# Attention heads stacked by DMA inside SBUF instead of by 0/1 matmuls

## The reference, cut to what matters

```python
q = (x @ Wq.T).reshape(B, T, h, dh).transpose(0, 2, 1, 3)      # first layer; k and v alike
att = jnp.einsum('bhqd,bhkd->bhqk', q, k) / jnp.sqrt(jnp.float32(dh))
out = jnp.einsum('bhqk,bhkd->bhqd', jax.nn.softmax(att, axis=-1), v)
x = x + out.transpose(0, 2, 1, 3).reshape(B, T, D) @ Wo.T
```

## Time and profile before

| | us |
|---|---|
| median of 3 runs | 3458.74 (3458.63 to 3459.36) |
| span of the profiled execution | 3458.2 |
| first attention, loop over 4 batches | 48.3 to 552.9 |
| causal attention, loop over 4 batches | 2846.0 to 3340.0 |
| TensorE busy | 2971.3 |
| mean granted TensorE clock | 0.937 |

### The profile page before, as it was taken

The page is one execution under the profiler, slowest core; times in us unless marked ns, Lnnn a source line. Parts: engine busy times, 40 slices in busy tenths (PEclk is TensorE's granted clock), DMA queues, the critical chain, the costliest instruction groups (busy, mean ns, idle before and its releaser), DMA issues. The chain is left out here.

```text
span 3458.2 us, 45847 instructions
## 1 busy us (share of the span) xinstructions
PE 2971.3 (86%) x13906; PEld 2032.8 (59%) x13906; DVE 1702.4 (49%) x4581; ACT 1078.2 (31%) x1834; POOL 1115.2 (32%) x1189
## 2 busy tenths in 40 slices
PE   5888888999999999999899999999999537777762
PEld 3544546887556556788766666666666425455552
DVE  3464463666655655566432332333333546546545
ACT  2443454443011001444333233333232014333410
POOL 1111105776444444676622222222223002213210
PEclk9999999999999999999999999999999659988985
DMA  3000002000000000200100000000000000000000
GB/s 138 1 0 0 0 0 92 0 0 0 1 0 0 0 0 0 98 0 0 61 1 1 1 1 1 1 1 1 1 1 1 34 0 1 1 0 0 0 0 24
DMA packets 5276, 39.97 MB, mean 12 GB/s; under 512 B 160, under 2 KB 4256, under 8 KB 4384
## 3 DMA queue, kind: packets, MB, share of 16 engines
q1 hardware_dynamic: 5152, 38.43, 2.7%
HBM read 36.33 MB, written 2.10 MB: 11 GB/s over the span
## 5 line engine op out<-in xcount | busy, mean ns | idle before, releaser
L364 PE MATMUL banks<-moe_parts 128*128 128x512 f32 x1536 | 370.0, 397 | 12.2 <-POOL moe_parts L444 7.3
L1500 PE MATMUL banks<-xt,back 128*128 128x512 f32 x768 | 349.6, 599 | 5.6 <-POOL lin L1725 5.6
L364 PEld LDWEIGHTS banks<-moe_parts 128*128 128x128 f32 x1536 | 289.2, 192 | 75.6 <-issue 17.2
L1749 POOL TENSOR_TENSOR back<-back,lin 128x256 f32<-128x256 f32 x112 | 110.4, 986 | 546.3 <-ACT lin L1623 546.0
L1647 DVE TENSOR_TENSOR back<-banks,lin 128x512 f32<-128x512 f32 x128 | 88.4, 691 | 396.1 <-PE banks L1511 396.1
L856 ACT ACTIVATE back<-banks 128x1024 f32<-128x1024 f32 (+3 forms) x256 | 212.7, 865 | 198.6 <-PE banks L736 197.5
L628 POOL TENSOR_TENSOR rounded<-back,rounded 128x1024 fp32r<-128x1024 f32 x36 | 85.3, 2370 | 572.2 <-ACT rounded L612 572.2
L718 PE MATMUL banks<-rounded 128*128 128x512 f32 (+3 forms) x512 | 181.9, 413 | 58.8 <-ACT rounded L612 14.5
L1500 PEld LDWEIGHTS banks<-xt,back 128*128 128x128 f32 x768 | 140.3, 191 | 151.9 <-issue 133.2
L896 DVE TENSOR_REDUCE back<-banks 128x1 f32<-128x512 f32 x256 | 159.1, 682 | 112.1 <-PE banks L718 110.5
L622 ACT ACTIVATE rounded<-banks 128x1024 fp32r<-128x1024 f32 x136 | 133.2, 1024 | 254.8 <-PE banks L599 254.8
(11 more groups left out here) (226 smaller groups left out, 5770.8 us busy)
## 6 DMA issues: line engine op xcount, KB each, us to landing
back<-p SPq DMA_DIRECT2D x1, 7696.0 KB, 21.6
ffn_pack<-ffn SPq DMA_DIRECT2D x1, 6144.0 KB, 29.2
back<-p SPq DMA_DIRECT2D x2, 2816.0 KB, 10.2
lin<-p_late SPq DMA_DIRECT2D x1, 5152.0 KB, 15.4
out<-x SPq DMA_DIRECT2D x1, 2048.0 KB, 7.5
x<-x_in SPq DMA_DIRECT2D x1, 1536.0 KB, 15.1
small_pack<-small SPq DMA_DIRECT2D x1, 619.0 KB, 4.8
x<-x_in SPq DMA_DIRECT2D x1, 512.0 KB, 3.7
```

Source lines behind the costliest of these rows:

```text
L364: mm = nc.tensor.matmul(bank[:], up[:, n % 2, a, which, kd, :], xp[:, b, kd, :], start=((a, b, kd) == (0, 0, 0)), stop=((a, b, kd) == (1, ...
L1500: mm = nc.tensor.matmul(bank[:], w[:, kd, pair * P:(pair + 1) * P], c.xt[:, kd, :], start=(kd == 0), stop=(kd == KD - 1))
```

## The change

`stack_heads` moves from TensorE to SyncE. For each head, operand and quadrant it issues one DMA of 32 partitions x 512 elements (64 KB) from `part` to `qs` or `ks`, 32 DMAs for a group, all on SyncE's queue and all behind one wait for `split`. Each group has a semaphore of its own (`c.stacked[hg]`). The 0/1 matrices, `keep_stacks` and their loads are gone. `qs` and `ks` hold four groups instead of two, and room is found by putting `pt` into the idle `ffn` region in the causal layer.

`keep_qk` of a group must now wait until the DMAs of the group before have read `part`. TensorE waits for `stacked[hg + 1]` ahead of the first scores of group hg+1. `qk` of groups 0 and 1 of the next batch moves to the ends of groups 2 and 3, and the next batch's `turn_xn` and latent move from group 3 to group 2. The prologue of each layer stacks groups 0 and 1 by DMA. After the loop SyncE waits for the last two stacks.

```diff
-    def stack_heads(pe, it, hg, parts_at, which=(0, 1)):
...
-                for hl in range(2):
-                    mm = nc.tensor.matmul(bank[:], stack_of[:, j, qk_, hl, :],
-                                          part[:, hl, qk_, :], start=(hl == 0),
-                                          stop=(hl == 1))
...
+    def stack_heads(sp, it, hg, k):
+
+        sp.wait_ge(c.split_ready.s, c.split_ready.at(it, k))
+        for which, dst, part_of in ((0, qs, (0, 0, 1, 1)), (1, ks, (0, 1, 0, 1))):
             for j in range(HJ):
...
+                for quadrant, hl in enumerate(part_of):
+                    sp.dma_start(dst[quadrant * HP:(quadrant + 1) * HP, hg, j, :].bitcast(F32),
+                                 part[j * HP:(j + 1) * HP, hl, which, :].bitcast(F32))\
+                        .then_inc(c.stacked[hg].s, 16)
+
+    def keep_qk(act, it, hg, k, in_loop=True):
+
         act.wait_ge(A.full.s, A.may_read(it, 2))
+        last = (hg - 1) % HG
+        if in_loop:
+            act.wait_ge(c.stacked[last].s, c.stacked[last].at(it, STACK * (2 if (hg, last) == (1, 0) else 1)))
...
                     if hg + 1 < HG:
                         turn_max(hg + 1)
-                    if hg + 2 < HG:
-                        stack_heads(pe, it, hg + 2, hg + 1)
                     values(hg, NT - 1)
-                    if hg + 3 < HG:
-                        qk(pe, it, hg + 3)
-                qk(pe, it, 0)
+                    if hg == 0:
+                        qk(pe, it, 3)
+                    if hg + 2 == HG:
+                        qk(pe, it, 0)
+                qk(pe, it, 1)
                 denominators(HG - 1)
...
                 pe.wait_ge(A.free.s, A.released(it, "y", NT - 1))
-                stack_heads(pe, it, 0, 3)
-                qk(pe, it, 1)
...
-                split(pool, it, 0)
+                    if hg == 0:
+                        split(pool, it, 3)
+                    if hg + 2 == HG:
+                        split(pool, it, 0)
+                split(pool, it, 1)
                 spread(HG - 1)
-                split(pool, it, 1)
+
+        @block.sync
+        def _(sp):
+            with sp.Fori(0, B) as it:
+                for k, hg in enumerate((2, 3, 0, 1)):
+                    stack_heads(sp, it, hg, k + 1)
+            for hg in (0, 1):
+                sp.wait_ge(c.stacked[hg].s, c.stacked[hg].at(B, STACK))
```

More of the change, by code:

```diff
@@ L563, in softmax_attention @@
     part = sb_r("part", [P, 2, 2, T], F32R)
-    qs = sb_r("qs", [P, 2, HJ, T], F32R)
-    ks = sb_r("ks", [P, 2, HJ, T], F32R)
+    qs = sb_r("qs", [P, HG, HJ, T], F32R)
+    ks = sb_r("ks", [P, HG, HJ, T], F32R)
     mx = sb("mx", [P, NT, HJ])
     mh = sb("mh", [P, NT, HJ], F32R)
-    stack = sb_r("stack", [P, 16 * P], F32R)
     v = sb("v", [P, NT, HG * HJ, HP])
     mp = sb("mp", [P, NT, P])
-    pt = sb("pt", [P, 4, 2, T])
+    pt = (c.carve(c.ffn, 0) if causal else sb)("pt", [P, 4, 2, T])
     os_ = sb("os", [P, HG, T])
@@ L613, in keep_qk @@
             .then_inc(A.free.s, 2)
[L615 to L623, removed]
     def split(pool, it, hg):
@@ L655, in _ @@
             w.wait_weights(act)
[L656 to L659, removed]
+            keep_qk(act, 0, 0, 1, in_loop=False)
+            keep_qk(act, 0, 1, 2, in_loop=False)
         @block.vector
@@ L687, in softmax_attention @@
         c.kt_ready.close(1)
-    A.open(HG * (2 + 2 * HJ + NT * HJ) + NT)
+    A.open(HG * (2 + NT * HJ) + NT)
+    for k in c.stacked:
+        k.open(STACK)
     D.open(KD + w.extra_uses + len(V_TILES) + HG * (NT * HJ + 3))
@@ L717, in scores @@
                         bank = D.fill("max", hg, qi, j)
-                        nc.tensor.matmul(bank[:, 0:n], qs[:, hg % 2, j, qi * P:(qi + 1) * P],
-                                         ks[:, hg % 2, j, 0:n], start=True, stop=True).then_inc(D.full.s, 1)
+                        nc.tensor.matmul(bank[:, 0:n], qs[:, hg, j, qi * P:(qi + 1) * P],
+                                         ks[:, hg, j, 0:n], start=True, stop=True).then_inc(D.full.s, 1)
                 def turn_max(hg):
@@ L804, in _ @@
                                 if (kt, pair) == (0, 0):
-                                    pe.wait_ge(A.free.s, A.released(it, "stack", hg + 1, 1, HJ - 1))
+                                    pe.wait_ge(c.stacked[hg + 1].s, c.stacked[hg + 1].at(it, STACK))
                                 scores(hg + 1, kt, (2 * pair, 2 * pair + 1))
@@ L808, in _ @@
                             values(hg, kt - 1)
-                        if hg + 1 == HG and kt == 0:
+                        if hg + 2 == HG and kt == 0:
                             turn_xn(nc, c, pe, it)
@@ L937, in _ @@
                             invert(hg - 1)
-                        if hg + 1 == HG and kt == 1:
+                        if hg + 2 == HG and kt == 1:
                             w.norm_latent(dve, it, c.ve)
@@ L996, in softmax_attention @@
         c.kt_ready.close()
+    for hg, k in enumerate(c.stacked):
+        k.close()
+        if hg < 2:
+            k.base += STACK
     c.set_up.base += 2
-    c.stack_ready.base += 1
-def stack_matrices(ap):
-    return ap.rearrange("p (j w h m) -> p j w h m", j=HJ, w=2, h=2)
 class MhaWeights:
@@ L1015, in __init__ @@
         self.wo = c.back[:, 2560:3584].rearrange("p (g m) -> p g m", g=HG)
-        self.stack = c.back[:, 3584:3584 + 16 * P]
     def memory(self, sb):
@@ L2070, in __init__ @@
         self.mask = take(T)
-        self.stack = take(16 * P)
     def memory(self, sb):
@@ L2317, in program @@
                     c.rounded = now.enter_context(nc.sbuf_tensor(f"rounded{n}", [P, rounded], F32R))
-                c.back = now.enter_context(nc.sbuf_tensor(f"back{n}", [P, BACK - (rounded or SCOPED)], F32))
+                c.back = now.enter_context(nc.sbuf_tensor(f"back{n}", [P, SBUF_LEFT - rounded if rounded else BACK - SCOPED], F32))
                 for layer, loads in layers:
```

68 lines of the change are left out of this document (24 added, 44 removed).

## The result

The changed kernel takes 3636.9 us, the median of 4 runs (3628.6 to 3639.2), against 3459.05 for the kernel before: 1.051 times as long, 95% interval 1.0495 to 1.0525. The profiled execution, the shortest of the four, has a span of 3626.7 us where it was 3458.2, and a mean granted clock of 0.888 where it was 0.937. The forecast of 3418 was wrong in its sign, and the range ended at 3505.

A forecast was written before the change was run, and what follows sets the result against it. A chain alternating between engines, with stacking on its path, was taken to bound the kernel. Savings of 44 and 37 us, less 32 for prologues and 8 for clock, gave 41 below 3458.2: forecast 3418 us, range 3380 to 3505.

The forecast's parts named there:

- The interval: On SyncE's queue, from one stacking DMA's start to the next: 0.40 us taken, between 0.38 and 0.54.
- D: Time from the end of GpSimd's subtraction to the landing of a group's last DMA: 14.5 us, bounds 12.4 and 18.8.
- The first rival: SyncE issues at its back-to-back pace, 0.48 us: D = 17.0, 59 us more, 3477, slower than before; chance 0.30.
- the point of decision at 0.455: SyncE's interval from which the 41 us of predicted saving are used up.
- The landing: Time for a stacking DMA's data to arrive after its instruction: 2.0 us taken, from 1.5 fixed in a store.
- the 0.1 of the wait: Allowance within D for the wait around a group's DMAs: 0.1 us.
- the data path with room: Stacking DMAs' data should not queue: 64 KB in 0.40 us is 164 GB/s, under half the 348 seen.
- The prologues: Before each attention's loop, waiting for stacking DMAs loses 13.0 us in the first and 19.4 in the causal, together 32.
- A batch of the first attention: Chain from first scores to next batch: 112.8 us instead of 125.6, saving 12.8 three times.
- The latent: In the causal attention, moving it into group 2 adds about 13.5 us there, much of it paid during waits for `part`.
- 1 us a batch for the clock: Matmuls running at a lower clock behind idle times cost 8 us in all, bounds 0 and 16.
- A causal batch by the chain: Causal attention's batch takes about 112 us, saving 11 three times and 3 in the last, 37 with rounding.

The follow-up runs named there:

- the last series: Kernel before plus six runs of 12 SyncE DMAs between and within SBUF and HBM: 0.46 and 0.45 us across, 0.66 within HBM, 0.63 within SBUF.
- with 16 DMAs: Against the changed kernel, q's and k's copies for one quadrant and head joined into one 128 KB DMA, 16 a group instead of 32: 3410.2 us, ratio 0.9859.
- the kernel with everything together: Against the changed kernel: 16 joined DMAs, quadrant 0's four ahead of the subtraction, group 1's other twelve in the prologue behind the barrier: 3374.9 us.

## Why the prediction was wrong

**The interval is the step that failed.** "I take 0.40, nearer to the lone ones", between 0.38 and 0.54. It is 0.635, above the upper bound. The rows that the bounds rest on the earlier trace rows are all copies between HBM and SBUF, and the last series shows that these are another kind, at 0.46. The reasoning that large loads had slowed them down was wrong too: 32x512 from HBM lasts 0.42 behind another, as the large loads' 0.43, and within SBUF size hardly enters from 1 to 256 KB. And a lone instruction lasts less than one behind another in both kinds (0.51 against 0.59 here), so a lone row could not price a queue of 32. Put into the prediction's own sum, 0.635 gives D = 21.8. The sum had 3531 at D = 18.8 and rises by about 29 us for each us beyond (54 us between its 3477 and 3531, for 1.86 us of D): 3531 + 3.0 x 29 = 3618. Measured 3637. So by the prediction's own slopes the interval explains about 200 of the 219 us of error. What is left hardly depends on D: measured less forecast is 23 us at a D of 12, 16 at 17 and 19 at 21.8.

**The first rival was the mechanism that happened**, issue on the path, past the point of decision at 0.455 and at a pace outside its range.

**What held.** The landing (2.0), the 0.1 of the wait, and the data path with room (97 GB/s). The prologues: 13.0 and 19.4 at D = 14.5, and two for each us of D, make 27 and 34; it was 29 and 30. A batch of the first attention by the prediction's slopes, 1.5 + 3 x 5.7 above 112.8, is 131 us; it was 129.8. That it fits so well is in part luck: group 2's copies began 17.5 us into the batch and not 20.5, the wait for group 3's stack was 3.5 us where a D of 21.7 gives about 5.6 by the chain, and three later stretches were 0.8 to 1.5 us longer than the chain has them. With 16 DMAs it was 112.6. So what the removed matmuls and copies free was sized right in the first attention: its loop with 16 DMAs is 48 us shorter than before (57.08 to the next layer at 513.58, against 504.6), where the prediction had 44 at D = 14.5 and a few more below. The latent costs 12.5 where 13.5 was taken, though the stretch without it is 18.6, not 16.6.

**What was mis-sized: the causal batch, its start and its clock.** I allowed 1 us a batch for the clock. A causal batch by the chain is 112 + 3 x 7.2 = 134 us, or 131 if the third wait is the 4.87 that the trace shows (at 3148.19) instead of 7.2, and it was 140.3. The rows show where most of these 6 to 9 us are. First, a start that is too early in the chain: the prediction had the first transposes 11.9 us in, with 4.0 us of stacking freed, and they come 14.4 us in (3092.00). The fourth of the first scores, before and after:

```profile
2969.50 0.47 PE L718 MATMUL banks<-rounded 128*128 128x128 f32 x1 [0.23 <-DVE back L892]
```
```profile
3080.15 0.47 PE L707 MATMUL banks<-rounded 128*128 128x128 f32 x1 [1.99 <-DVE back L875]
```

VectorE begins these maxima 2.2 us behind the scores, where it was 0.4, after 2.90 us in which it waited for nothing that the profile shows. They follow its last add of the batch before (over at 3076.82); in the kernel before, the stacking and the projection lay between. In the kernel with everything together the transposes come 14.3 us in as well. Second, the clock. The output matmuls of one batch, twelve of the same form, ahead of the wait for group 1's copies and behind it:

```profile
3197.36 2.84 PE L769 MATMUL banks<-back 128*128 128x256 f32 x12
3208.21 5.08 PE L769 MATMUL banks<-back 128*128 128x256 f32 x12 [8.02 <-ACT rounded L611]
```

That is 2.2 us, and the projections of groups 2 and 0 take 1.0 us more each than in the kernel with everything together. The granted clock of the causal loop is 0.73, where it was 0.89 before. In the kernel with 16 DMAs, two causal batches with the same work differ by 3.3 us at 0.79 and 0.74, and in the kernel with everything together three of them take 112.1 to 112.8 at 0.82. By these rows the late start is worth 2.5 us a batch and the clock about 4. No run tests either by itself, and the rest is open.

At a D of 12 another term was too small: no causal batch waits for group 0's stack any more, and group 1's projection is over 20.3 us behind the fourth transposes (2986.99 to 3007.32, with everything together), where the prediction had 14.6.

The figure of the Trainium skill in "DMA: Bandwidth & Descriptors" (512 cycles, an estimate of 0.43 us with the clock that "Trainium Kernel Development and Optimization" gives for SyncE) lies near the copies across, 0.43 behind another in the earlier trace rows and 0.46 from start to start in the last series, and not near those within SBUF, 0.59 and 0.63; here the measurement decides. The rule of the Trainium skill to join small transfers (the same page, "Rules for kernel authors") was right for this kernel: joining in pairs is worth 227 us. By the series the reason here is the instruction's issue, as 32 KB and 256 KB issue alike.

## What to carry to other kernels

Price a long row of DMA instructions by their count and by a row of their own kind (source and destination in the same memories, one right behind another): neither their size nor a load from HBM stands in for it. Then follow who holds the source tile until the last has landed, because its next writer, and the PSUM banks behind that writer, pay each further instruction. Join copies by patterns over several rows before moving work to a queue: the same idea that loses 5.1% with 32 instructions in a stack wins 1.4% with 16, and 2.3% when those that are ready early also go early.

## What the runs showed of the hardware

- DMA instructions within SBUF, one behind another: 0.58 to 0.62 us each and 0.63 to 0.66 from start to start, for 1 KB as for 256 KB, 16 partitions as 128, and any quadrant. Between SBUF and HBM 0.42 to 0.43 and 0.46; HBM to HBM 0.59 and 0.63 once it runs. The 6144 KB load of the kernel before, fifth in the queue, is far beyond this: its instruction lasted 8.14 us.
- A lone instruction within SBUF is shorter, 0.51 to 0.52 us in six of six. The first of a series is so too in most cases (0.48 to 0.54) and not in all (0.59, 0.62 and 0.68).
- SyncE's and ScalarE's queues issue side by side: 0.63 and 0.66 us at the same time, each for 32x512. SyncE's is no slower than alone; ScalarE's was not run alone.
- From the instruction to the landing within SBUF it is 1.7 to 1.9 us for 1 KB, 1.8 to 2.0 for 32, 2.0 for 64, 2.3 for 128 and 2.6 for 256, against 0.63 to 0.64 from one start to the next.
- Without the stacking matmuls the granted clock of the causal loop is lower: 0.89 before, 0.82 in the fastest kernel and 0.73 in the kernel after, with TensorE busy 77, 74 and 65% of the loop. Twelve output matmuls that take 2.84 us behind other matmuls take 5.08 behind an idle time of 8.02 us in the same batch. So part of what was removed is paid again by what stayed.
